# The order of the engines' lists in a fused attention and mixture-of-experts block: single operations moved along them

## The chip, the cores and the metric

The kernel runs on one core of a Trainium2 chip. The metric is device time in microseconds (us), the median of several executions. One execution was profiled; the profile counts from the first to the last instruction of the program (the span).

## The reference

The reference computes one gated block on 32 sequences of 64 tokens with 128 features, all in float32:

```python
x = x + tanh(g_xattn) * xattn(layernorm(x), ctx, ctx, Wq, bq, Wk, bk, Wv, bv, Wo, bo)   # 16 heads of 8, softmax over the 64 keys
x = x + tanh(g_ffn) * ffn(layernorm(x))
# ffn: logits = x @ router_w; scores = softmax(logits); the two experts with the largest scores + expert_bias
#      sum over the two of score * (silu(x @ w1[e]) * (x @ w3[e])) @ w2[e], plus the same with the shared sw1, sw2, sw3
```

There are 8 routed experts and a shared one. The kernel computes all nine for all tokens and weighs each result by the token's gate (zero for experts that the token didn't choose).

## The kernel before

The 2048 tokens are cut into four chunks `n` of 512 (four tiles of 128). Everything stays in SBUF between the steps. Each step is a small function, and each of the five engines has its list of calls of these functions, written out by hand in program order; an engine goes through its list strictly in order. Each function waits on semaphores for its inputs and for the buffers that it overwrites to be free. No list knows of the others: the order of the work on the chip follows from the four lists and the waits.

The way of one chunk, with the engine of each function:

- Norm: VectorE `x_stats`, `norm_var(n, 0)`; GpSimd (POOL) `inverse_root(n, 0)`, a power of -0.5; VectorE `norm_shift`; ScalarE `x_norm`, which applies shift and scale.
- Projections: TensorE `turn_x` (transposes), ScalarE `xT_out`, TensorE `queries`, ScalarE `spread_q` (four calls, bias and a mask that spreads the heads); TensorE `keys_values`, ScalarE `keys_out`, `values_out`. Chunk 0 does these in halves (a third argument 0 or 1 for `spread_q`, a second one for the others).
- Scores in four windows `w` for each chunk: TensorE `scores`; VectorE `quad_max`, `other_half`, `batch_max` (the maximum over the keys); POOL `spread_max`; TensorE `shift(n, w, 0 and 1)`, which subtracts that maximum in PSUM; ScalarE `probs(n, w, 0 and 1)`, the exponentials.
- Output in four tiles `t`: TensorE `attention` (products with the values, and the sums), VectorE `inverse` and `normalise`, TensorE `project_out`, VectorE `residual`, `x2_stats`.
- Second norm: VectorE `norm_var(n, 1)`, POOL `inverse_root(n, 1)`, VectorE `x2_norm`, TensorE `turn_x2`, ScalarE `x2T_out` (the high part of a split in two), VectorE `x2_low` (the low part).
- Router: TensorE `route`, VectorE `logits` to `top_two` with ScalarE `router_exp`.
- Nine experts `e`: TensorE `up1` and `up3`, each a product of three matmuls of 128x512; ScalarE `tanh_half`, VectorE `silu`, `hidden`; TensorE `down`; ScalarE `weigh` (the gate); POOL `add`. The last expert of the last chunk is closed by VectorE `finish`.

Buffers that tie the lists: `up1` and `up3` have one PSUM bank each in chunks 0 to 2 and two in chunk 3, so `up1(n, e)` waits for `silu` of the expert before and `up3(n, e)` for its `hidden`; `down` has one bank (two in chunk 3) and waits for `weigh` of the expert before. `th`, `sl`, `h` and `ys` have two buffers each, so `hidden` waits for the `down` of two experts before, and `weigh` for the `add` of two experts before. From chunk 1 on the scores have one place in PSUM, which `probs` must have read before the next window. `turn_x2` also waits for `keys_out` and `values_out` of the next chunk, which share the bank `M0`. Weights are split in a high and a low part at the start: `split_high1`, `split_high3` on ScalarE, `split_low1`, `split_low3` on POOL.

`spin_up(count, bank)` does products of zeros on TensorE whose result nobody reads (two instructions to a call); the list before has 52 of them in twelve places, all ahead of `route(0)`. `gates` on ScalarE is the tanh of the two gate parameters; `value_bias_out` on TensorE and `bias_out` on VectorE make the bias of the output projection.

In the profile an instruction has the line of its function: 1197 `scores`, 1206 `shift`, 1253 `turn_x2`, 1262 and 1264 `route`, 1269 to 1271 the three matmuls of `up1` and `up3`, 1310 `down`, 1319 `spin_up`.

Of the kernel before, what the change touches and what calls it, by code (L numbers as in the profile page):

```python
# [55 lines left out]
def block_program(nc, x, ctx_t, first_w, kv_w, rest_w, rows, w1, w2, w3, out):  # L56
    ctx = ExitStack()
    with ctx:
# [85 lines left out]
        AV = [bank("AV0"), bank("AV1")]  # L144
# [117 lines left out]
        def _(pool):  # L262
# [68 lines left out]
            inverse_root(2, 0)  # L331
            spread_max(1, 1)
            spread_max(1, 2)
            add(0, 0)
            spread_max(1, 3)
            add(0, 1)
            residual_in(3)
            inverse_root(3, 0)
            add(0, 2)
            spread_max(2, 0)  # L340
            add(0, 3)
            spread_max(2, 1)
            add(0, 4)
            inverse_root(1, 1)
            add(0, 5)
            spread_max(2, 2)
            add(0, 6)
            add(0, 7)
            spread_max(2, 3)
# [4 lines left out]
            add(1, 2)  # L354
            add(1, 3)
            spread_max(3, 1)
            add(1, 4)
            inverse_root(2, 1)
# [3 lines left out]
            spread_max(3, 2)  # L362
# [22 lines left out]
        def _(act):  # L385
# [120 lines left out]
            values_out(0, 1)  # L506
            x_norm(1)
# [48 lines left out]
            weigh(0, 1)  # L556
            keys_out(2, 1)
            values_out(2, 1)
            probs(1, 3, 0)
            probs(1, 3, 1)  # L560
            tanh_half(0, 4)
            weigh(0, 2)
            weigh(0, 3)
            x_norm(3)
            probs(2, 0, 0)
            probs(2, 0, 1)
            tanh_half(0, 5)
            tanh_half(0, 6)
            weigh(0, 4)
            probs(2, 1, 0)  # L570
            probs(2, 1, 1)
            tanh_half(0, 7)
            weigh(0, 5)
            weigh(0, 6)
            x2T_out(1)
            probs(2, 2, 0)
            probs(2, 2, 1)
            tanh_half(0, 8)
            weigh(0, 7)
            tanh_half(1, 0)  # L580
            weigh(0, 8)
            tanh_half(1, 1)
            xT_out(3)
            probs(2, 3, 0)
            router_exp(1)
            probs(2, 3, 1)
            spread_q(3, 0)
            spread_q(3, 1)
            spread_q(3, 2)
            spread_q(3, 3)  # L590
            weigh(1, 0)
            keys_out(3, 0)
            values_out(3, 0)
            tanh_half(1, 2)
            keys_out(3, 1)
            values_out(3, 1)
            weigh(1, 1)
            tanh_half(1, 3)
            weigh(1, 2)
            probs(3, 0, 0)  # L600
            tanh_half(1, 4)
            probs(3, 0, 1)
            weigh(1, 3)
            tanh_half(1, 5)
            weigh(1, 4)
# [1005 lines left out]
```

## Time and profile before

| | |
|---|---|
| median of 3 runs | 185.66 us (185.56 to 185.68) |
| the profiled execution | 185.64 us |
| its span | 183.8 us |
| busy in the span: TensorE, VectorE, ScalarE, POOL | 95%, 77%, 63%, 46% |
| mean granted TensorE clock | 0.998 of full speed |

TensorE's ends are modelled and its matmuls overlap, so a busy TensorE is not one at its peak; how long an operation holds it is best read from the start of one operation to the start of the next. The time of an execution is 1.8 us more than its span.

### The profile page before, as it was taken

Reading aid. Unit: us, or ns where it says so; the run is one execution under the profiler, and the core shown is the slowest. Engines: PE = TensorE matmul, PEld = TensorE weight load, DVE = VectorE, ACT = ScalarE, POOL = GpSimd, SP = SyncE. Lnnn points to the kernel's source line nnn. Section 1 sums busy time; section 2 is a strip of 40 time slices with the busy share of each in tenths; the row PEclk is TensorE's granted clock in tenths of the full one; section 3 lists DMA queues with packets and bytes.
Section 4 is the critical chain, followed back from the end, with each engine's and each line's share of the span. In section 5 each row is a group of like instructions: output and inputs, shape, how many; then the busy total and the mean of one; then the engine's idle time right before and its main releaser. Section 6 shows DMA issues by size and latency. Waiting matters only on the chain. (4 is left out here: it accounts for less than half of the span.)

```text
span 183.8 us, 5525 instructions
## 1 busy us (share of the span) xinstructions
PE 174.3 (95%) x2172; PEld 135.2 (74%) x2172; DVE 140.7 (77%) x368; ACT 115.0 (63%) x306; POOL 84.0 (46%) x76
## 2 busy tenths in 40 slices
PE   7998999999999999999999999999999989999982
PEld 7887577687677776687867878687757769888861
DVE  1338588897988988698886959988897786884562
ACT  3499888317587774646587765847146467588660
POOL 8221993742052850672502555545023474448551
PEclk9999999999999999999999999999999999999999
DMA  6894000000000000000010000000100000010001
GB/s 150 287 417 183 0 5 5 4 0 0 4 4 0 4 5 0 0 4 5 2 57 4 4 0 2 0 4 14 46 0 5 0 0 5 0 57 4 0 0 57
DMA packets 2761, 6.14 MB, mean 33 GB/s; under 512 B 304, under 2 KB 688, under 8 KB 2736
## 3 DMA queue, kind: packets, MB, share of 16 engines
q1 hardware_dynamic: 2304, 5.33, 8.0%
q10 hardware_dynamic: 432, 0.47, 1.1%
q8 instruction: 17, 0.28, 0.7%
q14 instruction: 8, 0.07, 0.1%
HBM read 4.75 MB, written 1.05 MB: 32 GB/s over the span
## 5 line engine op out<-in xcount | busy, mean ns | idle before, releaser
L294 POOL TENSOR_TENSOR acc<-ys,acc 128x512 f32<-128x512 f32 x31 | 39.8, 1283 | 30.1 <-ACT ys L450 30.1
L450 ACT ACTIVATE ys<-Y,gate 128x128 f32<-128x128 f32 x112 | 32.0, 372 | 15.1 <-PE Y L1310 14.8
L1310 PEld LDWEIGHTS Y<-W,h 128*128 128x128 f32 x256 | 32.8, 191 | 6.3 <-issue 2.5
L269 POOL TENSOR_TENSOR m_exp<-rest_in,m_all 128x512 fp32r<-128x512 f32 x16 | 16.7, 1048 | 42.4 <-DVE m_all L719 42.4
L1310 PE MATMUL Y<-W,h 128*128 128x128 f32 x256 | 34.3, 277 | 1.7 <-ACT ys L450 0.9
L439 ACT ACTIVATE th<-A 128x512 f32<-128x512 f32 x32 | 19.3, 603 | 17.9 <-PE A L1271 17.6
L829 DVE SCALAR_TENSOR_TENSOR sl<-th,A 128x512 f32<-128x512 f32 x32 | 21.8, 681 | 7.0 <-ACT th L439 6.7
L838 DVE SCALAR_TENSOR_TENSOR h<-A,sl 128x512 f32<-128x512 f32 x32 | 22.1, 690 | 5.0 <-PE A L1271 2.3
L699 DVE TRANSPOSE_TENSOR_REDUCE m_part<-SC 128x32 f32<-128x1024 f32 x14 | 17.4, 1246 | 6.5 <-PE SC L1197 6.5
L430 ACT ACTIVATE P<-SC 128x512 f32<-128x512 f32 x28 | 15.7, 596 | 9.9 <-PE SC L1206 9.9
L727 DVE RECIPROCAL rden<-AV 128x128 f32<-128x128 f32 x16 | 15.2, 949 | 1.7 <-PE AV L1228 1.6
L1269 PE MATMUL A<-x2h,W3h 128*128 128x512 f32 x32 | 15.2, 474 | 0.8 <-DVE h L838 0.8
L1197 PE MATMUL SC<-q_blk,kT 32*32 32x256 f32 x448 | 15.3, 380 | 0.4 <-ACT q_blk L419 0.3
L1269 PE MATMUL A<-x2h,W1h 128*128 128x512 f32 x32 | 14.7, 460 | 0.0
L1271 PE MATMUL A<-x2l,W1h 128*128 128x512 f32 x32 | 12.6, 395 | 0.0
L1271 PE MATMUL A<-x2l,W3h 128*128 128x512 f32 x32 | 12.6, 395 | 0.0
L1270 PE MATMUL A<-x2h,W1l 128*128 128x512 f32 x32 | 12.6, 394 | 0.0
L1270 PE MATMUL A<-x2h,W3l 128*128 128x512 f32 x32 | 12.6, 394 | 0.0
L277 POOL TENSOR_TENSOR rstd<-veps,minus_half 128x4 f32<-128x4 f32 x8 | 8.2, 1019 | 9.6 <-DVE veps L674 9.3
L1319 PE MATMUL AV<-spin 128*128 128x128 f32 x70 | 11.3, 319 | 1.2 <-DVE spin L873 1.2
L419 ACT ACTIVATE q_blk<-M,first_in 128x512 f32<-128x512 f32 (+1 forms) x16 | 10.6, 743 | 2.4 <-issue 2.4
L1319 PEld LDWEIGHTS AV<-spin 128*128 128x128 f32 x70 | 10.7, 231 | 1.8 <-DVE spin L873 1.2
(131 smaller groups left out, 331.9 us busy)
## 6 DMA issues: line engine op xcount, KB each, us to landing
W<-in_w SPq DMA_DIRECT2D x3, 576.0 KB, 9.5
xc<-in_x SPq DMA_DIRECT2D x4, 256.0 KB, 8.8
out_y<-acc SPq DMA_DIRECT2D x4, 256.0 KB, 2.0
ctxT<-in_ctx_t SPq DMA_DIRECT2D x3, 256.0 KB, 10.1
rest_in<-in_rest_w SPq DMA_DIRECT2D x1, 533.0 KB, 7.2
ctxT<-in_ctx_t ACTq DMA_DIRECT2D x1, 256.0 KB, 4.8
first_in<-in_first_w ACTq DMA_DIRECT2D x1, 133.0 KB, 3.4
kv_in<-in_kv_w SPq DMA_DIRECT2D x1, 128.0 KB, 4.1
```

The source lines that it names most:

```text
L269: pool.tensor_tensor(m_exp[u % 2][:].rearrange("p (k c) -> p k c", c=QUAD), eye.unsqueeze(1).to_broadcast([D, 16, QUAD]), m_all[u % 2][:, ...
L294: pool.tensor_tensor(acc[n % 2][:], ys[at % 2][:], (acc[n % 2] if e else x2[n])[:], ALU.add)\
L439: act.activation(th[at % 2][:], up_bank(n, e, 0), ACT.Tanh, scale=0.5).then_inc(th_ready, 1)
L450: last = act.activation(ys[at % 2][:, t, :], down_bank(n, e)[:, t * D:(t + 1) * D], ACT.Copy, scale=weight)
L699: dve.tensor_reduce(m_part[u % 2][:, 0:2, :].rearrange("p i k -> p (i k)"), score_banks(n, w)[:].rearrange("p (k c) -> p k c", c=QUAD), AX ...
L829: dve.scalar_tensor_tensor(out=sl[at % 2][:], in0=th[at % 2][:], scalar=1.0, in1=up_bank(n, e, 0), op0=ALU.add, op1=ALU.mult).then_inc(sl_ ...
L838: dve.scalar_tensor_tensor(out=h[at % 2][:], in0=up_bank(n, e, 1), scalar=0.5, in1=sl[at % 2][:], op0=ALU.mult, op1=ALU.mult).then_inc(h_r ...
L1269: pe.matmul(dst, hi, x2h[n % 2][:], start=True, stop=False)
L1270: pe.matmul(dst, lo, x2h[n % 2][:], start=False, stop=False)
L1271: return pe.matmul(dst, hi, x2l[n % 2][:], start=False, stop=True)
L1310: last = pe.matmul(down_bank(n, e)[:, t * D:(t + 1) * D], h[at % 2][:, t * D:(t + 1) * D], W2[:, e, :], start=True, stop=True)
L1319: pe.matmul(to[:, 0:D], spin[:], spin[:], start=True, stop=True)
```

## The change

Every engine keeps its functions, their operands and their waits. The lists of POOL, ScalarE, VectorE and TensorE hold the same calls as before in another order; the list of the DMA queue is as it was. Only the filler differs in number: `spin_up` has 41 products in eleven places, and not 52 in twelve. The diff, cut to the starts of the lists and to the places that the text speaks of:

```diff
--- before.py
+++ after.py
@@ -317,49 +317,49 @@
             spread_max(0, 1)
             residual_in(0)
             residual_in(1)
+            spread_max(0, 2)
+            spread_max(0, 3)
+            split_low3(0)
+            split_low3(1)
+            split_low3(2)
+            spread_max(1, 0)
             split_low1(0)
             split_low1(1)
-            spread_max(0, 2)
             split_low1(2)
-            split_low3(0)
-            spread_max(0, 3)
-            split_low3(1)
-            spread_max(1, 0)
+            inverse_root(0, 1)
+            spread_max(1, 1)
             residual_in(2)
-            split_low3(2)
-            inverse_root(0, 1)
             inverse_root(2, 0)
-            spread_max(1, 1)
             spread_max(1, 2)
+            spread_max(1, 3)
             add(0, 0)
...
@@ -491,169 +491,169 @@
             act.wait_ge(set_pool, 1)
             act.activation(table_in[:], minus_half[:], ACT.Exp)
             act.wait_ge(first_loaded, 16)
-            keys_out(0, 0)
             x_norm(0, 0)
-            keys_out(0, 1)
             x_norm(0, 1)
             xT_out(0, 0)
-            values_out(0, 0)
+            keys_out(0, 0)
+            gates()
             xT_out(0, 1)
             spread_q(0, 0, 0)
             spread_q(0, 1, 0)
             spread_q(0, 2, 0)
             spread_q(0, 3, 0)
             spread_q(0, 0, 1)
-            values_out(0, 1)
-            x_norm(1)
             spread_q(0, 1, 1)
             spread_q(0, 2, 1)
             spread_q(0, 3, 1)
-            gates()
-            split_high1(0)
+            x_norm(1)
+            values_out(0, 0)
             xT_out(1)
-            split_high1(1)
+            keys_out(0, 1)
             probs(0, 0, 0)
             probs(0, 0, 1)
             probs(0, 1, 0)
+            probs(0, 1, 1)
+            values_out(0, 1)
             spread_q(1, 0)
-            probs(0, 1, 1)
             spread_q(1, 1)
             spread_q(1, 2)
             spread_q(1, 3)
-            split_high1(2)
-            split_high3(0)
-            keys_out(1, 0)
             probs(0, 2, 0)
             probs(0, 2, 1)
+            keys_out(1, 0)
+            split_high3(0)
             split_high3(1)
-            values_out(1, 0)
+            split_high3(2)
             probs(0, 3, 0)
             probs(0, 3, 1)
+            split_high1(0)
+            split_high1(1)
+            values_out(1, 0)
+            split_high1(2)
+            probs(1, 0, 0)
+            probs(1, 0, 1)
             keys_out(1, 1)
             values_out(1, 1)
-            split_high3(2)
-            probs(1, 0, 0)
-            probs(1, 0, 1)
             x2T_out(0)
-            x_norm(2)
-            tanh_half(0, 0)
-            router_exp(0)
             probs(1, 1, 0)
             probs(1, 1, 1)
+            tanh_half(0, 0)
+            x_norm(2)
+            tanh_half(0, 1)
+            probs(1, 2, 0)
+            probs(1, 2, 1)
             xT_out(2)
-            tanh_half(0, 1)
+            router_exp(0)
+            tanh_half(0, 2)
             spread_q(2, 0)
             spread_q(2, 1)
             spread_q(2, 2)
             spread_q(2, 3)
-            tanh_half(0, 2)
-            weigh(0, 0)
-            probs(1, 2, 0)
-            probs(1, 2, 1)
+            probs(1, 3, 0)
+            probs(1, 3, 1)
             keys_out(2, 0)
             values_out(2, 0)
+            weigh(0, 0)
             tanh_half(0, 3)
             weigh(0, 1)
...
@@ -880,9 +880,9 @@
             norm_var(1, 0)
             norm_shift(1)
             quad_max(0, 0)
-            quad_max(0, 1)
             other_half(0, 0)
             batch_max(0, 0)
+            quad_max(0, 1)
             other_half(0, 1)
             batch_max(0, 1)
             bias_out()
@@ -890,42 +890,57 @@
             other_half(0, 2)
             batch_max(0, 2)
             quad_max(0, 3)
+            other_half(0, 3)
             inverse(0, 0)
             normalise(0, 0)
-            other_half(0, 3)
             batch_max(0, 3)
             inverse(0, 1)
+            normalise(0, 1)
             residual(0, 0)
             x2_stats(0, 0)
-            normalise(0, 1)
             quad_max(1, 0)
             other_half(1, 0)
+            batch_max(1, 0)
             residual(0, 1)
-            x2_stats(0, 1)
-            batch_max(1, 0)
             inverse(0, 2)
             normalise(0, 2)
             inverse(0, 3)
             normalise(0, 3)
             residual(0, 2)
+            x2_stats(0, 1)
             x2_stats(0, 2)
             residual(0, 3)
             x2_stats(0, 3)
             norm_var(0, 1)
-            x_stats(2)
-            norm_var(2, 0)
+            quad_max(1, 1)
             x2_norm(0)
-            quad_max(1, 1)
-            x2_low(0)
-            norm_shift(2)
             other_half(1, 1)
             batch_max(1, 1)
+            x_stats(2)
+            x2_low(0)
+            norm_var(2, 0)
+            norm_shift(2)
+            silu(0, 0)
+            hidden(0, 0)
+            quad_max(1, 2)
+            other_half(1, 2)
+            batch_max(1, 2)
             logits(0)
             logit_max(0)
+            silu(0, 1)
             logit_diff(0)
-            silu(0, 0)
-            hidden(0, 0)
+            inverse(1, 0)
+            normalise(1, 0)
+            inverse(1, 1)
+            normalise(1, 1)
+            hidden(0, 1)
+            quad_max(1, 3)
+            other_half(1, 3)
+            batch_max(1, 3)
             exp_sum(0)
+            silu(0, 2)
+            residual(1, 0)
+            residual(1, 1)
...
             silu(1, 6)
             hidden(1, 6)
             x2_norm(2)
             silu(1, 7)
+            quad_max(3, 2)
+            other_half(3, 2)
+            batch_max(3, 2)
             hidden(1, 7)
-            quad_max(3, 2)
             x2_low(2)
+            inverse(3, 0)
             silu(1, 8)
             hidden(1, 8)
-            other_half(3, 2)
-            batch_max(3, 2)
+            normalise(3, 0)
+            inverse(3, 1)
...
@@ -1330,227 +1330,226 @@
             pe.wait_ge(first_loaded, 16)
             keys_values(0, 0)
             keys_values(0, 1)
-            spin_up(2, AV[0])
             turn_x(0, 0)
-            spin_up(5, AV[0])
+            spin_up(3, AV[0])
             turn_x(0, 1)
             queries(0, 0)
             spin_up(1, AV[0])
-            value_bias_out()
             queries(0, 1)
             spin_up(4, AV[0])
             scores(0, 0)
             scores(0, 1)
-            spin_up(8, AV[0])
+            spin_up(4, AV[0])
             turn_x(1)
             spin_up(2, AV[0])
             shift(0, 0, 0)
             shift(0, 0, 1)
+            value_bias_out()
             queries(1)
+            spin_up(1, AV[0])
             shift(0, 1, 0)
+            shift(0, 1, 1)
             scores(0, 2)
-            shift(0, 1, 1)
-            spin_up(3, AV[0])
             scores(0, 3)
             attention(0, 0)
-            keys_values(1, 0)
+            attention(0, 1)
             shift(0, 2, 0)
             shift(0, 2, 1)
-            attention(0, 1)
+            keys_values(1, 0)
             project_out(0, 0)
             scores(1, 0)
             shift(0, 3, 0)
             shift(0, 3, 1)
-            keys_values(1, 1)
             project_out(0, 1)
+            spin_up(2, Y0)
             attention(0, 2)
             attention(0, 3)
-            spin_up(1, Y0)
-            project_out(0, 2)
             shift(1, 0, 0)
             shift(1, 0, 1)
+            project_out(0, 2)
+            spin_up(2, Y0)
             project_out(0, 3)
-            spin_up(1, Y0)
             scores(1, 1)
-            spin_up(9, Y0)
+            keys_values(1, 1)
+            spin_up(7, Y0)
             turn_x2(0)
-            spin_up(6, Y0)
-            route(0)
+            spin_up(5, Y0)
+            shift(1, 1, 0)
+            shift(1, 1, 1)
             up1(0, 0)
             up3(0, 0)
-            turn_x(2)
-            shift(1, 1, 0)
-            shift(1, 1, 1)
+            scores(1, 2)
+            route(0)
             up1(0, 1)
             up3(0, 1)
-            scores(1, 2)
-            queries(2)
-            down(0, 0)
             attention(1, 0)
-            up1(0, 2)
             attention(1, 1)
-            keys_values(2, 0)
             shift(1, 2, 0)
             shift(1, 2, 1)
+            up1(0, 2)
+            turn_x(2)
+            scores(1, 3)
+            queries(2)
+            project_out(1, 0)
+            project_out(1, 1)
+            up3(0, 2)
+            down(0, 0)
+            shift(1, 3, 0)
+            shift(1, 3, 1)
+            keys_values(2, 0)
             up1(0, 3)
-            project_out(1, 0)
-            scores(1, 3)
-            up3(0, 2)
+            scores(2, 0)
+            attention(1, 2)
...
+            up3(1, 6)
             up1(1, 7)
+            scores(3, 2)
+            down(1, 5)
             up3(1, 7)
+            turn_x2(2)
+            attention(3, 0)
+            up1(1, 8)
+            up3(1, 8)
             down(1, 6)
-            turn_x2(2)
-            scores(3, 2)
-            up1(1, 8)
-            down(1, 7)
-            up3(1, 8)
+            attention(3, 1)
             route(2)
...
-            up1(3, 5)
             up3(3, 5)
+            up1(3, 6)
             down(3, 4)
-            up1(3, 6)
+            up1(3, 7)
+            up3(3, 6)
+            up1(3, 8)
             down(3, 5)
-            up3(3, 6)
-            up1(3, 7)
             up3(3, 7)
             down(3, 6)
-            up1(3, 8)
             down(3, 7)
             up3(3, 8)
             down(3, 8)
```

In all, the diff takes 293 lines out of the four lists and puts 292 in at other places.

## Rows read from the trace of the kernel before

**Rows 1.** The page: TensorE's busy time, and its granted clock in 40 slices.

```profile
PE 174.3 (95%) x2172; PEld 135.2 (74%) x2172; DVE 140.7 (77%) x368; ACT 115.0 (63%) x306; POOL 84.0 (46%) x76
...
PEclk9999999999999999999999999999999999999999
```

**Rows 2.** Timeline of TensorE to 70 us: start, duration, instructions, idle before.

```profile
13.14 0.67 PE L1197 MATMUL SC<-q_blk,kT 32*32 32x256 f32 x16 [0.31 <-ACT q_blk L419]
...
17.42 0.65 PE L1165 MATMUL M<-first_in,xn 128*128 128x128 f32 x4 [0.51 <-ACT q_blk L419]
...
18.68 0.74 PE L1206 MATMUL SC<-m_exp,negr 128*128 128x512 f32 x2 [0.16 <-POOL m_exp L269]
...
36.83 2.27 PE L1319 MATMUL Y<-spin 128*128 128x128 f32 x18
39.35 0.63 PE L1253 MATMUL M<-first_in,x2n 128*128 128x128 f32 x4 [0.25 <-DVE x2n L684]
...
41.39 0.28 PE L1262 MATMUL M<-rwhl,x2h 128*128 128x16 f32 x1
...
42.30 0.48 PE L1269 MATMUL A<-x2h,W1h 128*128 128x512 f32 x1
```

**Rows 3.** Timeline of TensorE, 146 to 181 us.

```profile
156.85 0.48 PE L1269 MATMUL A<-x2h,W1h 128*128 128x512 f32 x1
...
157.63 0.40 PE L1269 MATMUL A<-x2h,W3h 128*128 128x512 f32 x1
...
158.33 0.40 PE L1269 MATMUL SC<-x2h,W1h 128*128 128x512 f32 x1
...
179.01 1.16 PE L1310 MATMUL Y<-W,h 128*128 128x128 f32 x8 [0.78 <-DVE h L838]
```

**Rows 4.** Timeline of ScalarE (ACT) to 62 us.

```profile
7.62 0.87 ACT L467 ACTIVATE xn<-xc,nshift,rstd 128x128 f32<-128x128 f32 x2
8.39 0.46 ACT L390 ACTIVATE kT<-AV,first_in 128x256 f32<-128x256 f32 x1
...
9.51 0.37 ACT L411 ACTIVATE xnT<-M 128x256 f32<-128x256 f32 x1
...
11.04 1.96 ACT L419 ACTIVATE q_blk<-A,first_in 128x256 f32<-128x256 f32 x4
```

**Rows 5.** Timeline of VectorE (DVE) to 62 us.

```profile
6.65 0.16 DVE L678 SCALAR_TENSOR_TENSOR nshift<-mv,rstd 128x4 f32<-128x4 f32 x1 [0.93 <-POOL rstd L277]
...
14.34 1.25 DVE L699 TRANSPOSE_TENSOR_REDUCE m_part<-SC 128x32 f32<-128x1024 f32 x1 [1.85 <-PE SC L1197]
15.51 1.21 DVE L699 TRANSPOSE_TENSOR_REDUCE m_part<-A 128x32 f32<-128x1024 f32 x1
```

**Rows 6.** Timeline of GpSimd (POOL) to 70 us.

```profile
17.58 2.06 POOL L269 TENSOR_TENSOR m_exp<-rest_in,m_all 128x512 fp32r<-128x512 f32 x2 [5.29 <-DVE m_all L719]
```

**Rows 7.** Waits: engine and line, releaser, us in total, times, longest.

```profile
DVE h L838 <- PE Y L1310: 1.2, 2, 0.8
...
PE Y L1310 <- ACT ys L450: 0.9, 2, 0.6
...
PE A L1269 <- DVE h L838: 0.8, 2, 0.6
PE Y L1310 <- DVE h L838: 0.8, 1, 0.8
```

**Rows 8.** Timeline of VectorE, 60 to 184 us.

```profile
73.14 0.69 DVE L838 SCALAR_TENSOR_TENSOR h<-A,sl 128x512 f32<-128x512 f32 x1
...
77.53 1.12 DVE L684 TENSOR_SCALAR x2n<-x,mv,rstd 128x128 f32<-128x128 f32 x4 [1.13 <-POOL rstd L277]
...
116.26 2.09 DVE L684 TENSOR_SCALAR x2n<-x,mv,rstd 128x128 f32<-128x128 f32 x4
```

**Rows 9.** Timeline of GpSimd, 110 to 160 us.

```profile
116.47 1.28 POOL L294 TENSOR_TENSOR acc<-ys,acc 128x512 f32<-128x512 f32 x1 [0.41 <-ACT ys L450]
```

**Rows 10.** Window 120 to 140 us: busy us of PE, PEld, DVE, ACT, POOL.

```profile
120.00:140.00 20.00, 19.75 (x274) 14.78 (x266) 17.49 (x45) 9.19 (x23) 6.00 (x6) 1.00 0.04 15
```

More of the change, by code:

```diff
@@ L936, in _ @@
             top_two(0)
-            silu(0, 1)
-            quad_max(1, 2)
-            other_half(1, 2)
-            batch_max(1, 2)
-            inverse(1, 0)
-            silu(0, 2)
-            normalise(1, 0)
-            inverse(1, 1)
-            normalise(1, 1)
-            hidden(0, 1)
-            residual(1, 0)
-            x2_stats(1, 0)
-            quad_max(1, 3)
-            other_half(1, 3)
-            batch_max(1, 3)
-            hidden(0, 2)
-            silu(0, 3)
-            residual(1, 1)
-            x_stats(3)
-            norm_var(3, 0)
-            x2_stats(1, 1)
-            hidden(0, 3)
-            silu(0, 4)
+            hidden(0, 2)
             quad_max(2, 0)
@@ L967, in _ @@
             inverse(1, 3)
-            normalise(1, 3)
-            residual(1, 2)
-            x2_stats(1, 2)
-            silu(0, 5)
+            silu(0, 3)
+            hidden(0, 3)
+            x_stats(3)
             quad_max(2, 1)
@@ L974, in _ @@
             batch_max(2, 1)
+            x2_stats(1, 0)
+            normalise(1, 3)
+            x2_stats(1, 1)
+            silu(0, 4)
+            hidden(0, 4)
+            residual(1, 2)
+            x2_stats(1, 2)
+            norm_var(3, 0)
+            residual(1, 3)
+            x2_stats(1, 3)
+            norm_var(1, 1)
+            silu(0, 5)
             hidden(0, 5)
-            residual(1, 3)
+            x2_norm(1)
+            norm_shift(3)
             silu(0, 6)
             hidden(0, 6)
-            x2_stats(1, 3)
-            norm_var(1, 1)
-            x2_norm(1)
+            x2_low(1)
             quad_max(2, 2)
+            silu(0, 7)
             other_half(2, 2)
             batch_max(2, 2)
-            silu(0, 7)
+            logits(1)
+            logit_max(1)
             hidden(0, 7)
-            x2_low(1)
             inverse(2, 0)
             normalise(2, 0)
+            logit_diff(1)
+            silu(0, 8)
             inverse(2, 1)
-            silu(0, 8)
+            normalise(2, 1)
             hidden(0, 8)
@@ L1010, in _ @@
             same_and_lower(1)
+            silu(1, 1)
+            hidden(1, 1)
+            residual(2, 0)
+            x2_stats(2, 0)
+            residual(2, 1)
+            x2_stats(2, 1)
             ahead(1)
@@ L1013, in _ @@
             top_two(1)
-            hidden(1, 1)
-            inverse(2, 2)
-            normalise(2, 2)
-            residual(2, 1)
-            x2_stats(2, 1)
+            silu(1, 2)
+            hidden(1, 2)
             quad_max(3, 0)
@@ L1021, in _ @@
             batch_max(3, 0)
-            silu(1, 2)
-            hidden(1, 2)
-            residual(2, 2)
-            x2_stats(2, 2)
+            inverse(2, 2)
+            normalise(2, 2)
+            silu(1, 3)
+            hidden(1, 3)
             inverse(2, 3)
             normalise(2, 3)
-            silu(1, 3)
-            hidden(1, 3)
             silu(1, 4)
@@ L1095, in _ @@
             hidden(2, 5)
+            silu(2, 6)
+            hidden(2, 6)
             x2_norm(3)
-            hidden(2, 6)
             silu(2, 7)
@@ L1410, in _ @@
+            shift(2, 1, 0)
+            shift(2, 1, 1)
             up1(0, 5)
-            attention(1, 2)
-            attention(1, 3)
-            shift(2, 0, 0)
-            shift(2, 0, 1)
-            project_out(1, 2)
             up3(0, 5)
-            scores(2, 1)
-            up1(0, 6)
             down(0, 4)
-            project_out(1, 3)
-            up3(0, 6)
-            shift(2, 1, 0)
-            down(0, 5)
-            shift(2, 1, 1)
-            up1(0, 7)
-            scores(2, 2)
@@ L1427, in _ @@
-            up3(0, 7)
-            down(0, 6)
-            turn_x2(1)
             attention(2, 0)
             attention(2, 1)
+            up1(0, 6)
+            up3(0, 6)
+            turn_x2(1)
+            scores(2, 2)
+            up1(0, 7)
+            up3(0, 7)
+            down(0, 5)
+            route(1)
+            up1(0, 8)
+            down(0, 6)
+            turn_x(3)
             shift(2, 2, 0)
-            down(0, 7)
             shift(2, 2, 1)
-            up1(0, 8)
             up3(0, 8)
+            queries(3)
@@ L1437, in _ @@
             scores(2, 3)
             up1(1, 0)
+            down(0, 7)
             up3(1, 0)
-            down(0, 8)
-            project_out(2, 0)
-            route(1)
-            up1(1, 1)
-            turn_x(3)
-            shift(2, 3, 0)
+            project_out(2, 0)
+            project_out(2, 1)
+            up1(1, 1)
+            up3(1, 1)
+            shift(2, 3, 0)
+            down(0, 8)
+            keys_values(3, 0)
             shift(2, 3, 1)
+            up1(1, 2)
+            up3(1, 2)
@@ L1447, in _ @@
             down(1, 0)
-            queries(3)
-            up3(1, 1)
-            project_out(2, 1)
-            up1(1, 2)
-            attention(2, 2)
-            keys_values(3, 0)
-            up3(1, 2)
             scores(3, 0)
             keys_values(3, 1)
+            attention(2, 2)
             down(1, 1)
-            project_out(2, 2)
-            attention(2, 3)
             up1(1, 3)
-            down(1, 2)
             up3(1, 3)
```

251 lines of the change are left out of this document (120 added, 131 removed).

## The prediction, made before the kernel was run

> **What bounds the kernel now.** I read the page first: TensorE is busy 95% of the span, at a granted clock of 9 tenths or more in all 40 slices [rows 1]. That share includes filler (`spin_up`), so the next view is TensorE's timeline, and the reader should look there at start-to-start distances. It has two parts. Up to 42.30 us, where the first expert product `up1(0, 0)` starts, TensorE is often only kept busy: 18 filler instructions, 2.27 us of them, stand ahead of `turn_x2(0)` alone [rows 2]. That part is set by the chain input norm, transposes, queries, scores, maximum, softmax, output projection, second norm, which runs through all engines. From 42.30 to `down(3, 8)` at 179.01 no filler is left, and products follow each other with no more than tenths between [rows 2, 3]: this part is TensorE's own work. After it comes a fixed end of 4.8 us (183.8 − 179.01). So a new order can gain in three ways: the chain up to `up1(0, 0)`, the price of going from one kind of work to another on TensorE, and the waits left in the second part.
>
> **Start of the chain.** Before, ScalarE does `keys_out(0, 0)` ahead of `x_norm(0, 0)`, `keys_out(0, 1)` between the two halves, and `values_out(0, 0)` ahead of `xT_out(0, 1)`. So `x_norm` starts at 7.62 although VectorE's `nshift` was done at 6.65 + 0.16 = 6.81, `xT_out(0, 0)` at 9.51 and the first `spread_q` at 11.04 [rows 4, 5]. The new list puts both `x_norm` halves first and both `values_out` behind `x_norm(1)`. A half costs 0.77 (8.39 − 7.62): 6.85 + 2 × 0.77 = 8.4. Then `xT_out(0, 0)` 8.5, `keys_out(0, 0)` and `gates` behind it, `turn_x(0, 1)` at 8.9, `xT_out(0, 1)` 9.5, and `spread_q(0, 0, 0)` at 9.95 when `queries(0, 0)` is done: 1.1 earlier. Four of them take 1.96 and end at 11.9, so `scores(0, 0)` starts at 11.9 and not at 13.14: 1.2 earlier. Four more end at 13.6; `x_norm(1)`, two halves, follows at once and ends at 15.15; `turn_x(1)` starts at 15.25 and not at 17.42: 2.2 earlier.
>
> **First maxima.** VectorE now finishes `other_half` and `batch_max` of window 0 before it starts `quad_max(0, 1)`. Before, that 1.2 us reduction stood between [rows 5]. `quad_max(0, 0)` moves with the scores from 14.34 to 13.1 and ends at 14.35; from the end of a `quad_max` to `spread_max` on POOL it was 0.86 (15.51 + 1.21 to 17.58), which makes 15.2; one `spread_max` takes 1.03 (2.06 for two) [rows 5, 6]: 16.25. TensorE has passed `turn_x(1)` and two spins by then, so `shift(0, 0)` starts at 16.3 and not at 18.68: 2.4 earlier.
>
> **To the second transpose.** From here I carried the list on with the same durations. POOL now makes the maxima of windows 2 and 3 ahead of the weight splits (`split_low3`, `split_low1`), which aren't needed before `up3` and `up1`, and TensorE has both `shift(0, 1)` ahead of `scores(0, 2)`. The links that wait last, in their order: `spread_max(0, 1)` ends at 18.2 (one `quad_max`, small reductions and `spread_max` behind the first), both `shift(0, 1)` at 18.9, `probs(0, 1, 1)` at 19.95, which lets `scores(0, 3)` start at 20.0; `quad_max(0, 3)` waits for that of window 2 and ends at 23.35, and with `inverse(0, 0)` and `normalise(0, 0)` ahead of its `batch_max`, which VectorE does in between, `spread_max(0, 3)` ends at 26.4; `shift(0, 3)` at 27.3, `probs(0, 3)` at 28.3. Then `attention(0, 2)` at 28.4, `attention(0, 3)` at 29.6 (behind `residual(0, 1)`, which now follows the maximum of window (1, 0)), the last `inverse` from 30.85, the last `project_out` at 32.2, the last `residual` to 33.35, `norm_var` to 34.2, the root on POOL to 35.3; `quad_max(1, 1)`, now ahead of it, holds `x2_norm(0)` to 35.5, and it ends at 36.6. `values_out(1, 1)`, for which `turn_x2(0)` waits too, ends at 36.6 as well, since `keys_values(1, 1)` went behind `scores(1, 1)`: this is what will be late next. `turn_x2(0)`: 36.7 against 39.35, 2.65 earlier. Behind it `x_stats(2)` now stands ahead of `x2_low(0)` on VectorE and costs 0.3. `norm_shift(2)` stands right behind `norm_var(2, 0)`, so VectorE stands while POOL ends `residual_in(2)` and its root; `silu(0, 0)`, queued behind it, couldn't start before that anyhow. `up1(0, 0)` starts at 39.0. In that 3.3 us gain `route(0)` isn't done yet (0.91, from 41.39 to 42.30), but `shift(1, 1)` is (at most 0.74 for the pair) [rows 2]: 3.3 − 0.91 + 0.6 = **3.0**, of which I take 2.9. Bounds: 2.0, if a link of this walk has a few more tenths, and 3.5, if the two ends at 36.6 come sooner.
> The eleven spins that are gone (52 to 41 calls, 0.25 each by the 18 instructions in 2.27) I cost at nothing: they ran only while TensorE waited. Without that cover, their price is the clock (below).
>
> **Changes of kind.** A product of three matmuls takes 0.70 from start to start when it follows another product at once (157.63 to 158.33), and 0.78 behind a `down` (156.85 to 157.63) [rows 3]. Counted in the two lists from `up1(0, 0)` on, neighbours of different kind fall from 144 to 129: up1 and up3 of an expert, two attentions, two projections now stand together. At 0.08 that is 15 × 0.08 = 1.2. Where only products gain (22 to 27 pairs) it is 0.4, so I take **0.8**, bounds 0.2 and 1.6.
>
> **Waits of the second part.** Those that the profile names on TensorE are 0.9 for `ys`, 0.8 and 0.8 for `h` [rows 7]; the last 0.8, ahead of `down(3, 8)`, stays, because the end of the lists is the same. The others stand where too little work lies between a producer and its reader. Counted in the lists with the starts above, the least work between two `up3` that share a bank was one product or less and is now at least 1.3 us; between `up3` and the `down` of the same expert it was 1.3 to 3 in many places and is now 3.2 or more in chunks 0 to 2. One `hidden` is 0.69 [rows 8]: it fits. So these waits should shrink, but the walk finds two new ones: `up3(1, 8)` behind `hidden(1, 7)`, which now has `quad_max(3, 2)` ahead of it (0.4), and `turn_x2(3)` behind `x2_norm(3)`. I take a gain of **1.0**; bounds a gain of 1.7 and a loss of 1.5.
> The second of these has a price that depends on POOL: `x2_norm` takes 1.12 where POOL is idle and 2.09 where an `add` runs beside it [rows 8, 9]. I count no more of that than before, where it was paid too. The Trainium skill, "SBUF — State Buffer", section "SBUF: two separate sides", says that one port pair is an exclusive lock between VectorE and GpSimd, and that the loser waits for the whole instruction. The rows agree; it speaks against any order that brings an `add` beside `x2_norm`, and would make that one of the rivals below.
>
> **Sum.** 2.9 + 0.8 + 1.0 = 4.7 us off the profiled execution's 185.64 (median of the runs 185.66): **180.9**. All upper bounds give 6.8 and 178.8.
>
> **Rivals.**
> *Only the start gains.* VectorE is busy 17.49 of 20 us between 120 and 140 [rows 10]; when TensorE wants its 20 us in 19, any bad order makes VectorE the bound. Then the later terms vanish: 185.6 − 2.9 = 182.7. Against it: my walk meets only tenths.
> *The lock.* Each of the three later `x2_norm` meets an `add` and lies open on the path to `turn_x2`: 3 × (2.09 − 1.12) = 2.9 on top, 183.8 [rows 8]. Against it: counted in the lists, 6.4 us or more of TensorE's work now stand between the last `project_out` of a chunk and its `turn_x2`, before 5 to 5.7.
> *All given back.* The walk misses a queue that stands across the start, like `weigh(0, 0)`, which waits for `top_two(0)` while `tanh_half(0, 3)` and the chain behind it are queued on ScalarE: 185.6. It needs a lost 3 us in one place.
> *Slower: a ring of waits.* The new order puts `down` further behind `up3`, but `h` has two buffers: `hidden(e)` must wait for `down(e − 2)`, VectorE stands in order, and the `silu` that TensorE's next `up1` needs is queued behind it. Before, that wait was 1.2 us in two places, up to 0.8 [rows 7]. With such a round in each of 27 experts the gain of 4.7 is gone from 0.17 us a round, and at 0.25 the time is 180.9 + 6.7 = 187.6. Against it: in the lists `down(e − 2)` still starts a microsecond or more ahead of most `hidden(e)`; `down(1, 6)` ahead of `hidden(1, 8)` is tight.
> *The clock.* All slices stand at the upper level, 2.4 GHz, with the filler in place [rows 1]. With fewer spins before 20 us, a fall to 1.2 GHz would double TensorE's work while it lasts; over 6 us that is up to 6 us, and 186 or so. Against it: my idle gaps are up to 0.7 us, against 0.51 ahead of `turn_x(1)` before.
>
> **How the numbers follow.** Forecast 0.60 (alone: 179.2 to 182.2), only the start 0.19, lock 0.04, given back 0.04, ring 0.09, clock 0.04. The measurement can tell about 0.2%, 0.37 us. Faster: 0.60 + 0.19 + 0.04 = 0.83; same 0.04; slower 0.09 + 0.04 = 0.13. From 178.8 to 184.2 the first three cases lie almost whole, which is 8 in 10.
>
> **What would show it.** The profile after should have the first `spread_q` near 10, `shift(0, 0)` near 16.3, `turn_x2(0)` near 36.7, `up1(0, 0)` near 39 and `down(3, 8)` near 174.3, with 135.3 us between these two. The prediction is wrong if `up1(0, 0)` isn't before 40.5, if waits of TensorE for `h`, `sl` or `ys` sum to over 4 us, or if the clock row drops early.

## The result, and the profile after

The new order takes 179.78 us (median; 179.73 to 179.84) against 185.67 on the same chip: a ratio of 0.968, with a 95% interval of 0.966 to 0.970. 180.9 had been forecast. Medians and ranges below are over all executions of a run; its ratio leaves out those that the chip ran slower at a lower granted clock, four in all. The profiled execution took 179.81 us with a span of 177.9, so the span is 5.9 us shorter and what lies around it is the same.

The page of the kernel after, busy time and granted clock (TensorE's, in tenths):

```profile
PE 169.3 (95%) x2150; PEld 133.1 (75%) x2150; DVE 141.3 (79%) x368; ACT 115.0 (65%) x306; POOL 84.4 (47%) x76
...
PEclk9999999999999999999999999999999999999998
```

VectorE, ScalarE and GpSimd do what they did [rows 1] within 0.6 us, in less time. TensorE has 22 matmuls fewer, the eleven spins of two each. Its clock stays at the upper level up to the last slice, in which its last matmul ends. Its timeline (start, duration, instructions, idle before) shows where the chain of the start has gone:

```profile
11.77 0.67 PE L1197 MATMUL SC<-q_blk,kT 32*32 32x256 f32 x16 [0.48 <-ACT q_blk L419]
...
15.12 0.63 PE L1165 MATMUL M<-first_in,xn 128*128 128x128 f32 x4 [0.47 <-ACT xn L467]
...
16.18 0.74 PE L1206 MATMUL SC<-m_exp,negr 128*128 128x512 f32 x2
...
35.18 1.73 PE L1319 MATMUL Y<-spin 128*128 128x128 f32 x14
36.98 0.63 PE L1253 MATMUL M<-first_in,x2n 128*128 128x128 f32 x4
...
39.37 0.39 PE L1269 MATMUL A<-x2h,W1h 128*128 128x512 f32 x1
...
41.88 0.28 PE L1262 MATMUL M<-rwhl,x2h 128*128 128x16 f32 x1
...
47.54 0.60 PE L1165 MATMUL M<-first_in,xn 128*128 128x128 f32 x4
```

Line for line with [rows 2]: the first scores are 1.37 us earlier, `turn_x(1)` 2.30, `shift(0, 0)` 2.50, `turn_x2(0)` 2.37, `up1(0, 0)` 2.93. Now look at the last two rows. `route(0)` comes behind the first product here, which the forecast had counted. `turn_x(2)`, the transpose of the third chunk, had no part in it: it comes 8.2 us behind `up1(0, 0)`, while in the old list it was the second call behind it.

The late part of the same timeline:

```profile
150.09 0.48 PE L1269 MATMUL A<-x2h,W1h 128*128 128x512 f32 x1
...
172.79 1.16 PE L1310 MATMUL Y<-W,h 128*128 128x128 f32 x8 [0.78 <-DVE h L838]
```

Against [rows 3], `up1(3, 0)` is 6.76 us earlier and `down(3, 8)` 6.22. From `up1(0, 0)` to `down(3, 8)` it is 133.42 us instead of 136.71: 3.29 less. The forecast had 135.3 there, 1.4 less: its terms of 0.8 and 1.0, less what `route(0)` takes more than `shift(1, 1)`. The waits of TensorE from the first expert product on (engine, line, releaser, us in total, times, longest), with VectorE's wait for a `down`:

```profile
PE Y L1310 <- DVE h L838: 0.8, 1, 0.8
PE M L1253 <- DVE x2n L684: 0.4, 1, 0.4
PE A L1269 <- DVE h L838: 0.2, 1, 0.2
```

```profile
DVE h L838 <- PE Y L1310: 0.5, 1, 0.5
```

The wait for `ys` is gone, that of `up3` for `h` is down from 0.8 to 0.2, and the ring of waits (`hidden` behind `down`) is 0.5 instead of 1.2 [rows 7]. At the end, VectorE and GpSimd:

```profile
174.31 1.13 DVE L847 SCALAR_TENSOR_TENSOR acc<-Y,tg,acc 128x128 f32<-128x128 f32 x4 [1.58 <-POOL acc L294]
```

```profile
171.51 2.68 POOL L294 TENSOR_TENSOR acc<-ys,acc 128x512 f32<-128x512 f32 x2 [0.31 <-ACT ys L450]
```

`finish` now waits for GpSimd's last two adds and not for the last `down`, so 5.1 us follow the start of `down(3, 8)` (177.9 − 172.79) instead of 4.8.

### The profile page after: what moved, and what is told of

Same layout as the page of the kernel before. It is cut to its first block and busy times, and to the rows that moved or that the text cites. A ratio compares the mean times of both kernels' runs of the same rounds, so it can differ in the third digit from the quotient of the medians.

```text
span 177.9 us, 5480 instructions
## 1 busy us (share of the span) xinstructions
PE 169.3 (95%) x2150; PEld 133.1 (75%) x2150; DVE 141.3 (79%) x368; ACT 115.0 (65%) x306; POOL 84.4 (47%) x76
## 5 line engine op out<-in xcount | busy, mean ns | idle before, releaser
L1310 PE MATMUL Y<-W,h 128*128 128x128 f32 x256 | 34.8, 279 | 0.8 <-DVE h L838 0.8
L1269 PE MATMUL A<-x2h,W3h 128*128 128x512 f32 x32 | 14.2, 445 | 0.2 <-DVE h L838 0.2
L1197 PEld LDWEIGHTS SC<-q_blk,kT 32*32 32x32 f32 x448 | 6.8, 104 | 6.2 <-issue 3.0
L1206 PE MATMUL SC<-m_exp,negr 128*128 128x512 f32 x28 | 9.9, 429 | 0.5 <-POOL m_exp L269 0.4
```

The source lines that it names most:

```text
L1197: last = pe.matmul(to[row:row + QUAD, i * 512 + t * HALF:i * 512 + (t + 1) * HALF], k[r:r + QUAD, pair + row:pair + row + QUAD], q[r:r + Q ...
L1269: pe.matmul(dst, hi, x2h[n % 2][:], start=True, stop=False)
L1310: last = pe.matmul(down_bank(n, e)[:, t * D:(t + 1) * D], h[at % 2][:, t * D:(t + 1) * D], W2[:, e, :], start=True, stop=True)
```

## Experiments

**Half of the lists each: the start.** All four lists of after up to the first expert product, those of before behind.

```diff
 TensorE: new list ..., shift(1, 1, 1)
+route(0)            # from here on the old list
+up1(0, 0), up3(0, 0), turn_x(2), up1(0, 1), ...
```

> The lists up to the first expert product in the new order, all behind it in the old one. If the change has two independent gains (start 2.6 to 2.9 us, rest 3.3), this kernel stands near 182.9 us, its first product near 39.4 and 136 to 137 us of the second part as before. If the start alone carries the gain, it is near 180; if the start's gain is given back in the second part by old waits, near 185.5.

185.64 us, a ratio of 0.9986 (0.9955 to 1.0016): no gain. The last of the three expectations came. The start itself kept its lead, `turn_x2(0)` at 37.02 and `up1(0, 0)` at 40.22, but at `up1(1, 0)` 0.3 us were left (85.80; before 86.11). TensorE and VectorE of this hybrid:

```profile
43.26 0.63 PE L1165 MATMUL M<-first_in,xn 128*128 128x128 f32 x4 [1.40 <-ACT xn L467]
```

```profile
41.18 0.16 DVE L678 SCALAR_TENSOR_TENSOR nshift<-mv,rstd 128x4 f32<-128x4 f32 x1 [1.14 <-POOL rstd L277]
```

`nshift` of chunk 2 is done at 41.3, and `x_norm(2)` follows on ScalarE. VectorE's same instruction before and, in the second fence, after:

```profile
41.25 0.15 DVE L678 SCALAR_TENSOR_TENSOR nshift<-mv,rstd 128x4 f32<-128x4 f32 x1
```

```profile
41.15 0.16 DVE L678 SCALAR_TENSOR_TENSOR nshift<-mv,rstd 128x4 f32<-128x4 f32 x1 [1.13 <-POOL rstd L277]
```

In time this chain hasn't moved at all. But that is the doing of the new lists too, which queue it later: VectorE starts `x_stats(2)` at 37.66 instead of 36.70, behind the maximum of window (1, 1), and GpSimd does `spread_max(1, 1)` and `residual_in(2)` between its two roots. GpSimd's root of chunk 2, before and after:

```profile
38.26 1.04 POOL L277 TENSOR_TENSOR rstd<-veps,minus_half 128x4 f32<-128x4 f32 x1 [0.37 <-DVE veps L674]
```

```profile
40.10 1.02 POOL L277 TENSOR_TENSOR rstd<-veps,minus_half 128x4 f32<-128x4 f32 x1
```

Before, the root was done at 39.30 and `nshift` stood in VectorE's list behind `x2_low(0)`. After, it waits for the root. No run has the new start with this chain in its old place.

The old list asks for the result as the second call behind `up1(0, 0)`, and `tanh_half(0, 0)` is queued behind `x_norm(2)` on ScalarE, so that `up1(0, 1)` waits another 0.48 for `silu`. So the lead of two microseconds is spent waiting for chunk 2.

**The same with a mended seam.** `turn_x(2)` behind `scores(1, 2)`, the first `tanh_half` and `silu` ahead of what waits for chunk 2.

```diff
 PE:  up1(0, 0), up3(0, 0)
-turn_x(2)
 up1(0, 1), up3(0, 1), scores(1, 2)
+turn_x(2)
 ACT: x2T_out(0)
+probs(1, 1, 0), probs(1, 1, 1), tanh_half(0, 0)
 x_norm(2)
+tanh_half(0, 1)
 DVE: norm_shift(2)
+silu(0, 0), hidden(0, 0)
 logits(0)
```

> The new lists up to up1(0,0) and the old ones behind, as in the hybrid that gave the start's gain back, with a mended seam: ScalarE gets the tanh of the first two expert products and the two probs of (1,1) ahead of x_norm(2), VectorE silu and hidden of (0,0) straight behind norm_shift(2), and TensorE turn_x(2) three products later, behind scores(1,2). Theory (the start's gain was lost only because the old lists ask for x_norm(2) at once, and the chain to it had not moved): up1(0,0) stays at 39.4 to 40.2, turn_x(2) no longer waits 1.4 us, and the median comes to 183.6 (185.7 less 2.1). Rival (the old lists behind are late at many places, so that an early start is worth nothing to them): 185.4 to 185.7, with the lead gone again by up1(1,0).

185.15 us, 0.9978 (0.9954 to 1.0002). The wait of 1.4 us is gone and two others stand there:

```profile
PE M L1170 <- ACT xnT L411: 0.8, 1, 0.8
PE A L1269 <- DVE sl L829: 0.7, 1, 0.7
```

`queries(2)` stands right behind `turn_x(2)` and waits for the copy between them; `up1(0, 1)` waits for `sl`. At `up1(1, 0)` 0.56 us of the lead are left (85.55). That is nearer to the rival than to the theory: a lead helps these old lists little.

**The other half: the rest.** The old lists up to `up1(0, 0)`, the new ones behind. The first version has `shift(1, 1)` ahead of `up1(0, 0)`, as the new list has.

> The lists up to the first expert product in the old order (with the old filler), all behind it in the new one. Two independent gains: near 182.4 us, the first product near 42.3, the second part 133 to 134 us. If the second part is shorter only because the start came sooner: near 185.6.

184.91 us (183.52 to 185.59), 0.9932 (0.9904 to 0.9960), between the two expectations. In the profiled execution (185.08) `up1(0, 0)` came 2 us late, at 44.31, since `shift(1, 1)` waited for GpSimd's `m_exp`, and the granted clock fell. Windows of this hybrid (busy us of PE, PEld, DVE, ACT, POOL with instructions, then the clock):

```profile
40.00:44.00 4.00, 3.08 (x24) 2.69 (x23) 2.07 (x7) 0.60 (x1) 1.05 (x1) 0.96 0.00 0
44.00:47.00 3.00, 3.00 (x8) 1.87 (x7) 0.54 (x1) 2.26 (x5) 0.00 (x0) 0.50 0.03 5
47.00:50.00 3.00, 3.00 (x63) 1.86 (x66) 2.52 (x6) 1.56 (x4) 0.00 (x0) 0.98 0.00 0
```

Hence a second version:

```diff
 PE: route(0)
-shift(1, 1, 0), shift(1, 1, 1)
 up1(0, 0), up3(0, 0)
+shift(1, 1, 0), shift(1, 1, 1)
```

> The old lists up to up1(0,0), the new ones behind, as in the first hybrid of that kind, but with shift(1,1) on TensorE behind up3(0,0) instead of ahead of up1(0,0), so that nothing at the cut waits for GpSimd's m_exp. Theory (the second part's 3.3 us are its own and need no early start): the granted clock stays at 1.0 at 40 to 50 us, up1(0,0) at 42.3, up1(1,0) near 85.7, down(3,8) near 175.7, median 182.4. Rival (the second part, too, gives its gain back when the start is the old one): above 184.

184.16 us, 0.9909 (0.9893 to 0.9924); the clock stayed up. From `up1(0, 0)` (42.72) to `down(3, 8)` (177.36) it is 134.64 us, 2.1 less than before, although the cut makes a wait of its own, for the `probs` behind the moved `shift`:

```profile
45.87 1.10 PE L1197 MATMUL SC<-q_blk,kT 32*32 32x256 f32 x32 [1.03 <-ACT P L430]
```

Without it the stretch would take 133.6 by this estimate, near after's 133.42. From `up1(1, 0)` (87.74) on it takes 89.62 us, as in after (89.64). So from there on the pace of the new lists needs no early start. But the theory's 182.4 did not come, and the median lies just above the rival's 184: from `up1(0, 0)` to `up1(1, 0)`, around the cut, it takes 45.02 us where after takes 43.78, and `up1(0, 0)` itself came 0.4 late.

**Later cuts.** New lists up to `up1(1, 0)`, old ones behind; then old lists up to `up1(2, 0)`, new ones behind.

```diff
 PE: new list ..., scores(2, 3)
+down(0, 7), up1(1, 0), up3(1, 0), down(0, 8), ...                   # old list
```

> The new lists up to up1(1,0), the old ones behind. Theory (gains of stretches add up when the cut falls where no late chain crosses it): up1(1,0) at 83.15, then the old lists' own pace; with 2.1 us of products drawn ahead (route(1), queries(3), turn_x(3)) and 0.8 left behind (down(0,7)) the median is 185.7 - 2.96 - 1.3 = 181.4, and what the new lists win behind the cut is 1.7 us. Rival (the old lists give the lead back, as in the hybrid cut at up1(0,0)): above 184.5.

```diff
 PE: old list ..., up3(1, 8), route(2)
+attention(3, 0), attention(3, 1), up1(2, 0), shift(3, 2, 0), ...    # new list
```

> The old lists up to up1(2,0), the new ones behind. Here attention(3,0) and (3,1), 1.9 us, come behind the cut and down(1,7), 0.8 us, is already done. Theory (of what the second part wins, some 1.8 us lie behind up1(2,0), in waits of TensorE for VectorE's h and ScalarE's ys): down(3,8) near 177.1, 1.9 ahead of before, median 184.1. Rival (the late stretch wins nothing by itself, the difference is work that the new lists had drawn ahead): down(3,8) at 178.5 or later, median above 185.2.

The first took 183.28 us, 0.9857 (0.9838 to 0.9876), 2.4 less than before and 3.5 more than after. That lies between its theory (181.4) and its rival (above 184.5). 0.7 of the 3.5 is a wait at the cut (`scores(2, 3)` for `P`); the rest, 2.8, is the most that the new order can win behind `up1(1, 0)`. The second took 186.59 us, 1.0051 (1.0034 to 1.0068): slower than before. TensorE at its cut:

```profile
126.22 0.47 PE L1269 MATMUL A<-x2h,W1h 128*128 128x512 f32 x1 [1.01 <-DVE sl L829]
...
129.48 0.50 PE L1269 MATMUL A<-x2h,W1h 128*128 128x512 f32 x1 [1.16 <-DVE sl L829]
```

VectorE at the same place:

```profile
124.40 0.96 DVE L727 RECIPROCAL rden<-AV 128x128 f32<-128x128 f32 x1 [1.65 <-PE AV L1228]
125.39 0.69 DVE L829 SCALAR_TENSOR_TENSOR sl<-th,A 128x512 f32<-128x512 f32 x1
```

Its new list has `inverse(3, 0)` ahead of `silu(1, 8)`; here the attention that it reads has only just been done, and the `silu` waits behind it. The rival's numbers came (`down(3, 8)` at 179.45), but the seam's two waits, 2.2 us, hide what the late stretch wins. From `up1(2, 0)` to `down(3, 8)` it is 53.2 us instead of 55.7; 1.9 of these 2.5 are the two `attention` calls that now stand ahead of it, and the second wait lies inside. What the late stretch wins alone stays open.

**ScalarE's order of the start alone.** First in the old lists, with the first two weight splits behind the moved calls and `value_bias_out` on TensorE behind `shift(0, 0)`; then taken out of the new ones.

```diff
 ACT of before:
-keys_out(0, 0)
 x_norm(0, 0)
-keys_out(0, 1)
 x_norm(0, 1), xT_out(0, 0)
+keys_out(0, 0), gates()
 ...
+x_norm(1), values_out(0, 0), xT_out(1), keys_out(0, 1), ...
```

> The lists of before, with ScalarE's alone in the new order up to values_out(0,1), split_high1(0) and (1) behind them, and value_bias_out on TensorE behind shift(0,0,1) as that order needs. Theory (ScalarE's order sets the first scores): scores(0,0) at 11.8 instead of 13.14. What becomes of it: if VectorE's and GpSimd's orders of the start carry nothing of their own, up1(0,0) comes 1.3 us earlier, near 41.0, and the median is 184.4; if the rest of the start is needed too, up1(0,0) stays within 0.4 us of 42.3 and the median is 185.4 to 185.7.

> The lists of after, with ScalarE's first 23 operations in the order of before. Theory (the 1.34 us at the first scores run through to the end, and nothing behind them has slack): scores(0,0) near 13.1, up1(0,0) near 40.7, median 181.1. Rival (behind the first scores the filler products and the waits take up the difference): up1(0,0) below 39.8 and a median below 180.2.

In the old lists: 189.69 us, 1.0193 (1.0158 to 1.0228). The profiled execution was the fastest of six, 187.81. Its loss of 2.1 us is one wait, because I had put the splits ahead of the `spread_q(1)` that frees a bank for `keys_values(1, 0)`:

```profile
26.97 0.67 PE L1148 MATMUL M<-ctxT,kv_in 128*128 128x256 f32 x2 [2.50 <-ACT q_blk L419]
```

The other five took 189.20 to 190.32 at a lower mean clock (0.976 to 0.991), and no profile shows where. So this run says nothing on the worth of the order for the whole time, except that up to there `scores(0, 0)` and `shift(0, 0)` were only 0.5 us ahead: `shift(0, 0)` waits for GpSimd's `m_exp` there. Taken out of the new lists: 181.74 us, 1.96 more than after (0.9777, 0.9757 to 0.9796); `turn_x(1)` waits again,

```profile
17.72 0.66 PE L1165 MATMUL M<-first_in,xn 128*128 128x128 f32 x4 [1.41 <-ACT q_blk L419]
```

and `up1(0, 0)` starts at 41.46, 2.09 later than in after; `down(3, 8)` at 174.89, 2.10 later. That is more than the theory's 181.1 and 40.7; 0.3 of the 2.09 may be a later beginning of this execution (its `scores(0, 0)` comes at 13.44, that of before at 13.14). In this run the delay of the start goes through to the end undiminished.

**Changes of kind.** Eight pairs of neighbours swapped in TensorE's list, which makes 140 neighbours of different kind from 129; all else as in after.

```diff
 up1(0, 1)
-up3(0, 1)
 attention(1, 0)
+up3(0, 1)
 attention(1, 1)
...
```

> The new order with eight swaps of two neighbours in TensorE's list (mostly an up3 and the down or attention behind it), which bring the neighbours of different kind in the second part from 129 back to 140. If a change of kind costs 0.08 us by itself, 11 x 0.08 = 0.9 us more than the new order's 179.8: 180.7, without new waits in the profile. If only waits matter and a change of kind is hidden: 179.8.

180.58 us (0.9710, 0.9686 to 0.9734), 0.80 more than after by the medians, 0.6 by the ratios, and in the profile `down(3, 8)` at 173.60, 0.81 later. The waits of TensorE behind `up1(0, 0)` are those of after, with the same amounts. So a change of kind costs 0.80 / 11 = 0.073 us in the mean. It is no even price: 0.79 of the 0.81 stands at `up1(1, 0)` already (83.94 against 83.15), behind six of the eleven changes, and the last four, behind `up1(3, 0)`, bring 0.16 (0.65 there, 0.81 at the end).

**No filler.** All spins behind the first ten left out; they compute nothing that the output needs.

```diff
 turn_x(0, 0)
-spin_up(3, AV[0])
 turn_x(0, 1)
 ...
-spin_up(7, Y0)
 turn_x2(0)
-spin_up(5, Y0)
```

> The new order without any spin_up but the first ten: 31 products of filler less. Filler that runs only while TensorE waits costs nothing, and the clock stays at its upper level with the work alone: 179.8. If the filler is what keeps the clock up, the granted clock falls before 40 us and the time is 181 or more.

181.76 us (180.76 to 183.82), 0.975 (0.970 to 0.980): 1.3 more than after by the ratios, 1.9 by the profiled execution (181.69). Windows of this kernel:

```profile
12.00:16.00 4.00, 2.20 (x68) 1.39 (x52) 3.05 (x7) 4.00 (x13) 1.22 (x2) 0.98 0.95 369
16.00:19.00 3.00, 2.80 (x7) 1.92 (x7) 1.57 (x7) 1.96 (x5) 1.55 (x3) 0.50 0.09 29
19.00:22.00 3.00, 3.00 (x74) 1.27 (x76) 0.93 (x1) 2.26 (x7) 2.15 (x2) 0.96 0.01 3
36.00:40.00 4.00, 1.29 (x6) 1.00 (x7) 3.84 (x19) 2.15 (x7) 1.99 (x3) 0.97 0.00 0
40.00:43.00 3.00, 3.00 (x15) 1.87 (x21) 1.42 (x4) 2.40 (x6) 1.55 (x2) 0.50 0.02 5
43.00:46.00 3.00, 3.00 (x45) 2.15 (x30) 2.45 (x6) 0.87 (x3) 0.00 (x0) 0.97 0.00 0
```

Two times TensorE had been partly idle (2.20 of 4 us, 1.29 of 4 us), and then the clock stood at the lower level, 1.2 GHz. `up1(0, 0)` comes 0.68 later than in after, `up1(1, 0)`, behind the second fall, 2.04 (40.05 and 85.19). With the filler, the clock row of after stands at 9 tenths up to the last slice, so the filler is what holds the clock up in this order.

**The new wait that had been foreseen.** `quad_max(3, 2)` and what follows it put behind `hidden(1, 7)`.

```diff
 silu(1, 7)
+hidden(1, 7)
 quad_max(3, 2), other_half(3, 2), batch_max(3, 2)
-hidden(1, 7)
 x2_low(2)
```

> The new order with quad_max, other_half and batch_max of window (3, 2) behind hidden(1, 7) on VectorE instead of ahead of it. The wait of up3(1, 8) for hidden(1, 7), 0.5 us in the profile of the new order, should go: 179.8 - 0.4 = 179.4. If TensorE then waits elsewhere for the later maximum (shift(3, 2)) or later steps absorb it: 179.8.

> The lists of after with quad_max, other_half and batch_max of (3,2) behind hidden(1,7), a second time, with more rounds. Theory (the 0.46 us that the profile of the first run gained at up3(1,8) runs through to the end): median 179.3. Rival (it is given back): 179.8.

The first time 179.73 us (179.29 to 181.67), 0.9677 (0.9640 to 0.9713); the second time 179.57 (179.24 to 179.88), 0.9661 (0.9646 to 0.9676). In both profiles `down(3, 8)` comes 0.5 us earlier (172.33 and 172.21), so the wait was real and can be had; in the times the interval overlaps that of after. It is the fastest version here, by less than these runs can tell.

## Why the prediction was right, by its own steps

**What bounds the kernel**: right. TensorE stays busy 95%, and its starts move in the chain of the start and in its own list behind it.

**Start, 2.9**: right, link by link. Walked and measured: `spread_q` 9.95 (9.70), scores 11.9 (11.77), `turn_x(1)` 15.25 (15.12), `shift(0, 0)` 16.3 (16.18), `turn_x2(0)` 36.7 (36.98), `up1(0, 0)` 39.0 (39.37). With `route(0)` still to do (0.91) and `shift(1, 1)` done (0.57, from 38.80 to 39.37) the gain is 2.93 − 0.91 + 0.57 = 2.6. That the gain needs ScalarE's order is shown by the run that takes it out of the new lists: 1.96 us. Alone in the old lists it brought `shift(0, 0)` only 0.5 of 2.5 us, so the other lists' orders are needed as well.

**Changes of kind, 0.8**: the mean price was right, 0.073 against 0.08, though not even. By the mean, 15 × 0.073 = 1.1, an estimate, within the bounds.

**Waits of the second part, 1.0**: too small, the largest miss of the sum. The waits that the profile names behind `up1(0, 0)` went from 2.8 (0.9 + 0.8 + 0.8 from [rows 7], and 0.3 for `x2n`) to 1.4. The second part is 3.29 shorter although it holds 0.34 more work (0.91 − 0.57): 3.63. Less 1.1 for the kinds and 1.4 for named waits, 1.1 is left. With it the waits are 2.5, beyond the upper bound of 1.7. Of the two new waits foreseen, that ahead of `up3(1, 8)` was there and its removal moved `down(3, 8)` by 0.5; that for `x2n` is 0.4 in the list.

TensorE's list of waits shows only part of such a wait, because it counts from the modelled end of the last matmul. `up3(1, 8)` in after:

```profile
115.73 0.40 PE L1271 MATMUL A<-x2l,W1h 128*128 128x512 f32 x1
116.35 0.50 PE L1269 MATMUL A<-x2h,W3h 128*128 128x512 f32 x1 [0.23 <-DVE h L838]
```

From start to start this is 0.62. With the maximum behind `hidden(1, 7)`, in the last experiment, it is 0.23 at the same place: 0.39 were lost, and the list names 0.23 of them. The weight loads (PEld), which overlap with matmuls, name more. Those of `up1` and `up3`, before and after:

```profile
PEld A L1269 <- DVE h L838: 2.9, 7, 0.8
PEld A L1269 <- DVE sl L829: 1.6, 5, 0.4
```

```profile
PEld A L1269 <- DVE h L838: 0.9, 2, 0.7
```

With 0.2 for `sl` after, that is 4.5 us in twelve places and 1.1 in three. The 1.1 left over can lie there; how much of these waits delayed TensorE's starts isn't shown.

**The end**: taken as unchanged, it is 0.3 longer, for GpSimd's adds. Measured sum: 2.93 + 3.29 − 0.3 = 5.9, the span's difference, against 4.7. (Here `route(0)` and `shift(1, 1)` count where they stand; with the forecast's terms it is 2.6 + 3.63 − 0.3.)

**Spins removed, at nothing**: the clock row shows no price for the eleven that went; no run puts them back. That the rest could go too would have been wrong by 1.3 to 1.9 us. The rival of the clock had the right mechanism, but with the filler that is left the clock did not fall.

**The lock**: half of its condition came, an `add` beside each of the three; that they lie open on the path did not, nor did the price. VectorE after:

```profile
35.72 1.11 DVE L684 TENSOR_SCALAR x2n<-x,mv,rstd 128x128 f32<-128x128 f32 x4
...
70.84 2.13 DVE L684 TENSOR_SCALAR x2n<-x,mv,rstd 128x128 f32<-128x128 f32 x4
...
110.90 2.13 DVE L684 TENSOR_SCALAR x2n<-x,mv,rstd 128x128 f32<-128x128 f32 x4
...
144.20 2.04 DVE L684 TENSOR_SCALAR x2n<-x,mv,rstd 128x128 f32<-128x128 f32 x4
```

Each of the three long ones meets an `add` of GpSimd (at 71.09, 110.90 and 144.12). That is one more than before, where the one at 77.53 took 1.12 [rows 8], and the forecast had counted no more. Yet TensorE waits only 0.4 us for `x2n` in all, so the work put ahead of `turn_x2` covers it, as the argument against this rival said. The Trainium skill, "SBUF — State Buffer", section "SBUF: two separate sides", names the lock; the durations agree.

**What isn't borne out is that the terms can be had one by one.** The prediction added them so, and the rival "only the start gains" gave 182.7 for the start in front of a second part that wins nothing. The hybrid with just that took 185.64. By the medians the start alone gives 0.2 us (0.3 by its ratio) or, with its seam mended, 0.6 (neither interval excludes that there is no gain), the rest alone 1.6, both together 5.9. What is shown: the chain of chunk 2 stands at 41.2 with the old start and with the new one, which queues it later, and a list that asks for it early waits there. The new list has 8.2 us of other work ahead of it. The hybrids also pay for their cuts, 0.7 to 2.2 us in waits at each, since every list takes for granted what the others have done by then; so the shares are good to a microsecond or two. 3.7 is missing (5.9 less 1.6 and at most 0.6). The waits named at the two mended cuts are 1.5 and 1.0, so 2.5 of it may be the cuts' own doing; how much is stays open, and with it whether the terms add. The sum itself came out low by 1.2, inside its range, for the waits of the second part.

## What to carry to other kernels

When a chain is made earlier, look for the next chain that has not moved with it, or was queued later: the gain is kept only if TensorE's list has finished operands to work on until that one arrives. An order over several queues is one object: a stretch of one good order put beside a stretch of another can be slower than both, so price a stretch from the trace of the whole and take hybrids as rough, with the waits at their cuts beside them. Spins that fill an idle stretch should be costed by the clock that they hold up (1.3 to 1.9 us here), not by the time that they take.

## What the hardware showed unexpectedly

With TensorE busy 3.08 of 4 us ahead of it, the granted clock fell to 0.50 for about 3 us (44 to 47 us in the first hybrid of the rest), as it did after emptier stretches in the kernel without filler (2.20 and 1.29 of 4 us). In all three cases TensorE was busy 2.80 to 3.00 of the 3 us at 0.50, and the clock was back near 1.0 in the next window.

The busy share ahead doesn't settle it. In the profiled execution with the wait of 2.50 us at 26.97, TensorE was busy 1.50 of the 4 us from 23 to 27, and the clock stood at 1.00 there and up to 33 us. In the first hybrid of the start it was busy 2.49 of the 4 us from 40 to 44, and the clock stood at 1.00 there and up to 47 us. One kernel seems to do both: of the ten executions of the first hybrid of the rest, the three fastest (183.52 to 183.68 us) had a mean granted clock of 0.993 to 1.0, the profiled one 0.982 at 185.08. What decides it isn't shown here.
